# Attention in a macaron layer: the two narrowest diagonal key blocks as one step, the two narrowest maxima blocks in shared banks

## The chip, the cores and the metric

One core of one Trainium2 chip. The metric is the time of one launch on the device in microseconds. Before the change: 1210.66 us, median of 3 runs (1209.63 to 1210.69).

## The reference

Four sequences of 1024 tokens, 512 channels, 16 heads of 32 channels, fp32. A half-weighted feedforward, attention, and the half-weighted feedforward again, each after a layernorm without scale:

```python
x = x + 0.5 * ffn(layernorm(x), weight, bias)
x = x + attn(layernorm(x), Wqkv, bqkv, Wo, bo)
x = x + 0.5 * ffn(layernorm(x), weight, bias)
# ffn: w = clip(round(weight / mean|weight|), -1, 1) * mean|weight|;  x @ w.T + bias
# attn: kqv = x @ Wqkv + bqkv, 16 heads
#   scores = k q^T / sqrt(32); of the 1024 x 1024 the upper triangle is kept,
#   below it -10000; softmax over the axis that is summed against v (causal)
#   out = attn^T v;  out @ Wo + bo
```

## The kernel before

Everything runs in one program in which each engine's order is fixed by tables of rows. A sequence is a batch `b` (4 of them); its heads come in 4 head groups `g` of 4 heads. A head group's attention is done in 2 chunks `c` of 512 queries (`CW`), and a chunk in steps, one for each block of 128 keys up to the diagonal: 4 steps for chunk 0, 8 for chunk 1, `STEPS` = 12. Each step is a slot. 192 slots follow a head of 19 rows, and 10 tail rows follow them.

In a slot TensorE (PE) does, in this order:
- the scores of the step (`scores`, L1137): for each of 4 heads 3 matmuls of split operands (high and low parts), 32 rows of the array per head, so that four heads run side by side, into 4 banks of PSUM; then one matmul per head that adds the row of maxima (L1143);
- the values of the step before (`values`, L1159): 4 matmuls, each head into its own 32 partitions of bank 7;
- a block of maxima (A, L1107): 128 queries against up to 512 keys of the next head group (12 slots hold the 12 blocks of a group), again 3 matmuls for each of 4 heads, into 4 banks;
- then what the row of the table names: P is a piece of K or Q (12 matmuls of 512 columns, L1047), V a tile of values, O an output projection, F1 and F2 the feedforwards (8 matmuls, L1072), T1, T2, T3 transposes (L1064), M and N transposes of maxima and inverses, C the spread of inverses over the heads.

On ScalarE (ACT) a slot has the exponentials of its scores (`exponentials`, L981, one instruction per head, from PSUM to `prob`), high parts of what was multiplied, and the exponentials of the maxima block with their sums (`block_sums`, L953). VectorE (DVE) takes the maxima (`maximum`, L800), low parts (`low`), normalisations, residuals and layernorm statistics. GpSimd (POOL) zeroes the part of `prob` past the diagonal with an affine select (L701), adds biases and computes the inverse roots. SyncE (SP) issues the DMAs: loads and stores of x, weights, and the rows of maxima and inverses (`rows`, `inverse_rows`), which go from 16 partitions to the layout that L1143 and C read.

Seven banks form a ring. Scores take 4, an A block 4, other uses 1. A use waits in `bank_free` until the holder of its bank is done with it: of eight banks for scores and A one is shared in a slot, so that A's fourth bank waits for the first exponential of the slot's own scores, and the next scores' fourth bank for the first maximum of A. `prob` has two buffers, so exponentials of step n wait for the values of step n-2.

Diagonal steps are narrower. In `scores` a block is computed at least 256 queries wide, and an A block at least 256 keys wide:

```python
c, kb = (0, i) if i < QPC else (1, i - QPC)   # step_of
return c, kb, max(0, P * kb - CW * c)
off = min(off, 2 * P)                          # scores
n = CW if kc < c else max(2 * P, P * (r + 1))  # A blocks
```

So the last two steps of a chunk have scores of 256 and 256, exponentials of 256 and 128, values of 256 and 128 columns. The first two diagonal A blocks have matmuls of 256 and maxima of 128 and 256.

Of the kernel before, what the change touches and what calls it, by code (L numbers as in the profile page):

```python
# [30 lines left out]
STEPS = QPC + 2 * QPC  # L31
# [4 lines left out]
VG = GROUPS - 1  # L36


def step_of(i):

    c, kb = (0, i) if i < QPC else (1, i - QPC)
    return c, kb, max(0, P * kb - CW * c)


def diagonal(i):
    c, kb, _ = step_of(i)
    return kb >= QPC * c


def maxima(b, g, c):  # L50

    return [("A", b, g, QPC * c + r, kc) for r in range(QPC) for kc in range(c + 1)]


def pieces(b, g):
    return [("P", b, g, K_, 0), ("P", b, g, Q_, 0), ("P", b, g, K_, 1), ("P", b, g, Q_, 1)]
# [10 lines left out]
    "N P | A",  # L67
    "M P | A | X3.0",
    "P | A | X3.1",
    "C O.0 | A | X3.2",  # L70
    "O.1 | A",
    "N T3.0 O.2 | A | X3.3",
    "M F2.0 | A",
    "T3.1 O.3 | A | X3.4",
    "F2.1 | A",
    "T3.2 O.4 | A",
    "F2.2 | A",
)
GROUP1_ROWS = (
    "C P | A",  # L80
    "N P | A",
    "M P | A | X3.5",
    "P | A",
    "C T3.3 O.5 | A | X3.6",
    "F2.3 | A",
    "N T3.4 O.6 | A | X3.7",
    "M F2.4 | A",
    "T3.5 O.7 | A",
    "T3.6 F2.5 | A | X1.0",
    "T3.7 F2.6 | A | LV",  # L90
    "F2.7 | A",
)
GROUP2_ROWS = (
    "C P | A | X1.1",
    "N T1.0 P | A | X1.2",
    "M F1.0 | A | X1.3",
    "P | A | X1.4",
    "C T2.0 T1.1 P | A | X1.5",
    "T1.2 F1.1 | A | X1.6",
    "N T1.3 F1.2 | A | X1.7",  # L100
    "M T2.1 T1.4 F1.3 | A",
    "T1.5 F1.4 | A",
    "T2.2 T1.6 F1.5 | A",
    "T1.7 F1.6 | A",
    "T2.3 F1.7 | A",
)
GROUP3_ROWS = (
    "C T2.4 P | A",
    "N T2.5 P | A",
    "M T2.6 V.0 | A",  # L110
# [4 lines left out]
    "M V.3 | A",  # L115
    "V.4 | A",
    "V.5 | A",
    "V.6 | A",
    "V.7 | A",
)  # L120
FIRST_ROWS = (
    "P | A",
    "N P | A | | W",
    "M P | A",
    "P | A | | W",
    "C | A",
    "V.4 | A | | W",
    "N V.5 | A",
    "M V.6 | A | | W",
    "V.7 | A",  # L130
    " | A | | W",
    " | A",
    " | A | | W",
# [3 lines left out]
    "N | A",  # L137
    "M | | X3.0",
# [5 lines left out]
    "T3.1 F2.0",  # L144
    "O.3 | | X3.5",
# [33 lines left out]
    "V.3 | A A A",  # L179
# [73 lines left out]
BLOCKS = {u: n for n, u in enumerate([u for u in USES if u[0] == "A"])}  # L253
# [58 lines left out]
def macaron_kernel(nc, x, wqkv, bqkv, wo, bo, wf, bf, out):  # L312
    with ExitStack() as ctx:
# [309 lines left out]
        def _(pool):  # L623
# [65 lines left out]
            for k, s in enumerate(SLOTS):  # L689
# [4 lines left out]
                if s.step is not None:  # L694
                    i = s.step % STEPS
                    if diagonal(i):
                        n = step(s.b, s.step)
                        off = step_of(i)[2]
                        part = prob[:, n % 2, :, off:off + P]
                        pool.wait_ge(s_exp, 4 * n + 4)  # L700
                        nc.gpsimd.affine_select(out=part, in_=part, compare_op=ALU.is_ge, fill=0.0, base=0,  # L701
                                                pattern=[[0, 4], [1, P]], channel_multiplier=-1).then_inc(masked, 1)
# [11 lines left out]
        def _(dve):  # L714
# [75 lines left out]
            def maximum(u):  # L790

                _, b, g, qb, kc = u
                c, r = qb // QPC, qb % QPC
                n, off = (CW, 0) if kc < c else (P * (r + 1), CW - P * r)
                dve.wait_ge(ring_full, full(u))
                for h in range(4):
                    at = 4 * h + r
                    if BLOCKS[u]:
                        dve.wait_ge(a_free, block_at(u, h) - 4)
                    nc.vector.tensor_tensor_reduce(masked_scores[:, h, 0:n], psum(u, h)[:, 0:n], mask[:, off:off + n],  # L800
                                                   -SCALE, BIG, ALU.add, ALU.min, mst[:, c + kc, at:at + 1])\
                        .then_inc(a_max, 1)
# [7 lines left out]

            def inverse(u):

                _, b, g, c = u
                at = group(b, g)
                if c == 0:
                    dve.wait_ge(a_free, block_at(maxima(b, g, 0)[-1]))
                    of = ssum[:, 0, :]
                else:
                    dve.wait_ge(shift_exp, at)
                    nc.vector.tensor_tensor(msh[:, :, :], msh[:, :, :], ssum[:, 1:3, :], ALU.mult).then_inc(inverse_done, 1)  # L820
                    dve.wait_ge(inverse_done, 4 * at - 2)
                    nc.vector.tensor_tensor(msh[:, 0, :], msh[:, 0, :], msh[:, 1, :], ALU.add).then_inc(inverse_done, 1)
                    dve.wait_ge(inverse_done, 4 * at - 1)
                    of = msh[:, 0, :]
                if ended(u):
                    dve.wait_ge(ring_full, full(("N", b, g, c - 1) if c else ("N", *before(b, g), 1)))
                nc.vector.reciprocal(rcol[:, :], of).then_inc(inverse_done, 1)
# [36 lines left out]
            for k, s in enumerate(SLOTS):  # L864
# [27 lines left out]
        def _(act):  # L892
# [38 lines left out]
            def evacuate(u):  # L931
# [9 lines left out]
                act.wait_ge(value_done, step(b, g * STEPS + (STEPS if c else QPC)))  # L941
                nc.scalar.activation(chunk(b, CHUNKS * g + c), accv[:, :], ACT.Identity).then_inc(accv_free, 1)

            def block_sums(u, heads):

                _, b, g, qb, kc = u
                c, r = qb // QPC, qb % QPC
                n = CW if kc < c else P * (r + 1)
                for h in heads:
                    at = 4 * h + r  # L950
                    act.wait_ge(a_max, block_at(u, h))
                    of = masked_scores[:, h, 0:n]
                    nc.scalar.activation(of, of, ACT.Exp, bias=mst[:, c + kc, at:at + 1], scale=-1.0,  # L953
# [246 lines left out]
```

## Time and profile before

| | |
|---|---|
| median of 3 runs | 1210.66 us |
| the profiled execution | 1212.57 us |
| its span, first to last instruction | 1210.8 us |
| mean granted TensorE clock | 0.952 |
| slots (steps) | 192 |

A page of a profile gives the busy time of each engine, as microseconds and share of the span. The table of stretches gives the same for parts of the span, with the granted clock of TensorE as a share of 2.4 GHz. A timeline lists instructions merged by line: where they start, how long until the last of them ends, and in brackets how long the engine had been idle and what ended that. Ends of matmuls overlap the starts of the next, so a stage is measured from start to start.

### The profile page before, as it was taken

The numbers are of one execution on the slowest core, as the hardware profiler recorded it, in microseconds if no ns is written. First come the engines' busy times: TensorE is split into PE (matmuls) and PEld (weight loads), VectorE is DVE, ScalarE is ACT, GpSimd is POOL, SyncE is SP. The second block draws the span as 40 slices with busy tenths as digits, with TensorE's granted clock in tenths as the row PEclk, the third lists the DMA queues.
The fourth block names the chain that finished last, engine by engine and source line by source line (L and its number), as shares of the span: only waits on it lengthen the run. The fifth ranks groups of instructions, "written<-read, shape, count | busy, mean of one in ns | idle before, by whom it ended". The sixth has DMA issues, their size and how long they took to land.

```text
span 1210.8 us, 26364 instructions
## 1 busy us (share of the span) xinstructions
PE 1143.3 (94%) x9466; PEld 718.4 (59%) x9466; DVE 750.1 (62%) x2304; ACT 946.1 (78%) x2699; POOL 347.0 (29%) x503
## 2 busy tenths in 40 slices
PE   4688999899999999999999999999999999998996
PEld 3465556465666666665666666665666666654555
DVE  6865434479844666779745666779744666654344
ACT  1248887888888888888888888888888888888541
POOL 4821120035401232335401232335301332301243
PEclk9898978789999999999999999999999999997599
DMA  7431311011112211231112211330112212100121
GB/s 252 150 102 54 106 44 48 29 54 54 38 45 71 72 38 54 83 122 54 46 38 71 72 37 61 115 104 33 46 37 71 72 37 72 37 3 2 37 68 38
DMA packets 41969, 77.72 MB, mean 64 GB/s; under 512 B 5488, under 2 KB 11632, under 8 KB 41840
## 3 DMA queue, kind: packets, MB, share of 16 engines
q1 hardware_dynamic: 41840, 76.04, 18.8%
q8 instruction: 76, 1.25, 0.4%
q14 instruction: 53, 0.43, 0.1%
HBM read 49.81 MB, written 25.17 MB: 62 GB/s over the span
## 4 chain that ended last, share of the span: by engine, by line
PE 76%; DVE 10%; ACT 8%; issue 2%; POOL 2%; DMA 1%; SPq 0%; DVEq 0%; ACTq 0%; POOLq 0%
PE bank L1047 27%; PE bank L1107 14%; PE bank L1137 11%; PE bank L1159 10%; PE bank L1072 7%; ACT masked_scores L953 5%; DVE masked_scores L800 4%; PE bank L1064 3%; PE bank L1143 3%; DVE st L749 1%; DVE hn L768 1%; ACT prob L981 1%; DVE qT L776 1%; DVE xt L788 1%; ACT qT L904 1%
## 5 line engine op out<-in xcount | busy, mean ns | idle before, releaser
L800 DVE CUSTOM_DVE_ANT_0 masked_scores<-bank,mask 128x512 f32<-128x512 f32 (+3 forms) x768 | 382.1, 554 | 297.9 <-PE bank L1107 263.2
L953 ACT ACTIVATE masked_scores<-masked_scores,mst 128x512 f32<-128x512 f32 (+3 forms) x768 | 463.7, 610 | 48.1 <-DVE mst L800 47.5
L981 ACT ACTIVATE prob<-bank 128x512 f32<-128x512 f32 (+3 forms) x768 | 311.9, 491 | 40.2 <-PE bank L1143 39.2
L1107 PE MATMUL bank<-kT,qT 32*128 32x512 f32 (+2 forms) x2304 | 203.6, 404 | 14.9 <-ACT prob L981 8.4
L701 POOL TENSOR_SCALAR_AFFINE_SELECT prob<-prob 128x512 f32<-128x512 f32 x128 | 81.5, 637 | 448.5 <-ACT prob L981 447.5
L1107 PEld LDWEIGHTS bank<-kT,qT 32*128 32x128 f32 x2304 | 115.1, 191 | 159.3 <-issue 71.9
L1047 PE MATMUL bank<-hT,wqk 128*128 128x512 f32 x768 | 197.4, 407 | 0.0
L1137 PE MATMUL bank<-qT,kT 32*128 32x512 f32 (+2 forms) x2304 | 185.9, 394 | 5.2 <-DVE mst L800 4.5
L1047 PEld LDWEIGHTS bank<-hT,wqk 128*128 128x128 f32 x768 | 143.2, 193 | 37.6 <-ACT prob L981 7.1
L1137 PEld LDWEIGHTS bank<-qT,kT 32*128 32x128 f32 x2304 | 105.8, 192 | 83.5 <-issue 57.2
L1159 PE MATMUL bank<-prob,v 128*32 128x512 f32 (+3 forms) x1344 | 149.4, 518 | 0.0
L953 ACT ACTIVATION_READ_ACCUMULATOR masked_scores<-masked_scores,mst 128x1 f32 x768 | 148.3, 193 | 0.0
L1072 PE MATMUL bank<-wfT,hts 128*128 128x512 f32 x512 | 136.5, 410 | 1.4 <-DVE hts L774 1.4
L1072 PEld LDWEIGHTS bank<-wfT,hts 128*128 128x128 f32 x512 | 93.6, 193 | 23.9 <-DVE hts L774 2.4
L1047 PE MATMUL bank<-wvo,hts 128*128 128x512 f32 x384 | 99.9, 411 | 5.8 <-POOL hts L674 5.8
L667 POOL TENSOR_TENSOR xt<-xt,hb 128x512 f32<-128x512 f32 x64 | 82.1, 1283 | 60.6 <-DVE hn L768 60.6
L1047 PE MATMUL bank<-wvo,hT 128*128 128x512 f32 x384 | 99.2, 408 | 0.0
L1047 PEld LDWEIGHTS bank<-wvo,hts 128*128 128x128 f32 x384 | 72.5, 195 | 26.1 <-ACT prob L981 6.5
L1047 PEld LDWEIGHTS bank<-wvo,hT 128*128 128x128 f32 x384 | 71.8, 194 | 19.8 <-ACT prob L981 4.0
L918 ACT ACTIVATE hts<-bank 128x512 fp32r<-128x512 f32 x64 | 38.6, 603 | 56.9 <-PE bank L1064 36.0
L1064 PE MATMUL bank<-ident,hn 128*128 128x128 f32 x384 | 61.5, 291 | 19.7 <-DVE hn L768 19.3
L1143 PE MATMUL bank<-mneg,onesr 2*128 2x512 f32 (+2 forms) x768 | 77.8, 358 | 0.0
(87 smaller groups left out, 1008.8 us busy)
## 6 DMA issues: line engine op xcount, KB each, us to landing
wqk<-weight_scratch SPq DMA_DIRECT2D x30, 512.0 KB, 3.3
wvo<-weight_scratch SPq DMA_DIRECT2D x20, 512.0 KB, 6.0
xt<-in_L_attn_x_dram SPq DMA_DIRECT2D x32, 256.0 KB, 3.6
residual_scratch<-xt SPq DMA_DIRECT2D x32, 256.0 KB, 2.0
xt<-residual_scratch SPq DMA_DIRECT2D x32, 256.0 KB, 2.8
out_dram<-xt SPq DMA_DIRECT2D x32, 256.0 KB, 2.0
o<-in_L_attn_Wqkv_dram SPq DMA_DIRECT2D x12, 256.0 KB, 4.7
weight_scratch<-o SPq DMA_DIRECT2D x6, 512.0 KB, 2.9
```

Of the source, the lines that this page charges most:

```text
L667: nc.gpsimd.tensor_tensor(to, to, (bo2 if l == 1 else hb)[:, :], ALU.add).then_inc(xb_done[l], 1)
L701: nc.gpsimd.affine_select(out=part, in_=part, compare_op=ALU.is_ge, fill=0.0, base=0, pattern=[[0, 4], [1, P]], channel_multiplier=-1).the ...
L800: nc.vector.tensor_tensor_reduce(masked_scores[:, h, 0:n], psum(u, h)[:, 0:n], mask[:, off:off + n], -SCALE, BIG, ALU.add, ALU.min, mst[:, ...
L953: nc.scalar.activation(of, of, ACT.Exp, bias=mst[:, c + kc, at:at + 1], scale=-1.0, accum_out=ssum[:, c + kc, at:at + 1]).then_inc(a_free, 1)
L981: nc.scalar.activation(prob[:, at % 2, h, off:CW], psum(("S", b, n), h)[:, off:CW], ACT.Exp, scale=SCALE)\
L1047: m = nc.tensor.matmul(psum(u), left(x, k), right(y, k), start=(n == 0), stop=(n == len(terms) - 1))
L1064: m = nc.tensor.transpose(psum(u)[:, P * k:P * k + P], hn[:, TURN[u] % 2, P * k:P * k + P], ident[:, :])
L1072: m = nc.tensor.matmul(psum(u), h[:, part, k, :], wfT[:, k, :], start=(k == 0 and part == HI), stop=(k == KC - 1 and part == LO))
L1107: m = nc.tensor.matmul(psum(u, h)[:, 0:n], query_piece(b, g, c)[row, x, P * r:P * r + P], kT[g % 2][row, y, CW * kc:CW * kc + n], start=(t ...
L1137: nc.tensor.matmul(psum(u, h)[:, off:CW], kT[g % 2][row, x, P * kb:P * kb + P], query_piece(b, g, c)[row, y, off:CW], start=(term == 0), s ...
L1143: m = nc.tensor.matmul(psum(u, h)[:, off:CW], onesr[row, :], mneg[row, c, off:CW], start=False, stop=True)
L1159: m = nc.tensor.matmul(accv[HD * h:HD * h + HD, off:CW], v_of(b, g, kb, h), prob[:, at % 2, h, off:CW], start=(kb == 0), stop=(kb == QPC * ...
```

## The change

The last two key blocks of a chunk, (2, 3) and (6, 7), become one step. The 4 banks of its scores hold the later block's 256 queries in columns 0 to 255 and the earlier block's in 256 to 511; one exponential per head covers columns 128 to 511, one affine select on POOL zeroes both triangles, and the values follow as 4 matmuls of 256 and 4 of 128 columns. The maxima blocks of the first two diagonal query tiles share 4 banks in the same manner, with a maximum and a sum for each tile as before. A head group has 10 slots and 10 A blocks where it had 12, a launch 160 slots. The tables are written anew: uses of the two dropped rows are spread over the others, some rows hold two products, the first piece of the next weights comes in the last row of a group, N and M share a row. On DVE the first half of the inversion (`combine`) moves from N's slot to that of the second C. Number and size of the matmuls stay.

```diff
-STEPS = QPC + 2 * QPC
+KEYS = [[(0,), (1,), (2, 3)], [(0,), (1,), (2,), (3,), (4,), (5,), (6, 7)]]
+QUERIES = [[(0, (0, 1)), (0, (2,)), (0, (3,))],
+           [(0, (0,)), (0, (1,)), (0, (2,)), (0, (3,)), (1, (0, 1)), (1, (2,)), (1, (3,))]]
+STEPS = sum(CHUNK_STEPS)
...
+    return first_query(c, keys[0]) if len(keys) == 1 else P
...
-    return [("P", b, g, K_, 0), ("P", b, g, Q_, 0), ("P", b, g, K_, 1), ("P", b, g, Q_, 1)]
+    second = (Q_, K_) if g == 0 else (K_, Q_)
...
 GROUP2_ROWS = (
-    "C P | A | X1.1",
-    "N T1.0 P | A | X1.2",
...
+    "C T1.0 F2.7 P | A | X1.3",
+    "N M T1.1 F1.0 P | A | X1.4",
...
-                        part = prob[:, n % 2, :, off:off + P]
+                        part = prob[:, n % 2, :, at:at + m * P].rearrange("p h (m q) -> p h m q", m=m)
...
+                    for j, r, at, n, off in block_tiles(u):
+                        nc.vector.tensor_tensor_reduce(masked_scores[:, h, at:at + n], psum(u, h)[:, at:at + n],
...
+                        for j, r, at, keys, _ in block_tiles(u):
+                            n = max(HALF, keys)
+                            for h in range(4):
+                                if term == 0 and j == 0:
+                                    bank_free(u, h)
...
+                parts = [(kb, min(first_query(c, kb), HALF), HALF - HALF * j if len(keys) > 1 else first_query(c, kb))
+                         for j, kb in enumerate(keys)]
                 for term, (x, y) in enumerate(((HI, HI), (LO, HI), (HI, LO))):
+                    for kb, off, at in parts:
+                        for h in range(4):
...
+                for j, kb in enumerate(keys):
+                    off = first_query(c, kb)
+                    of = off - HALF * j
+                    for h in range(4):
+                        m = nc.tensor.matmul(accv[HD * h:HD * h + HD, off:CW], v_of(b, g, kb, h),
```

PE, the end of batch 1's last head group: the last two steps of chunk 1, before. L1137 are scores, L1143 the row of maxima, L1159 values, L1107 an A block, L1047 a product.

```order
L1137 MATMUL bank<-qT,kT 128x256 x12
L1143 MATMUL bank<-mneg,onesr 128x256 x4
L1159 MATMUL bank<-prob,vx 32x384 x4
L1107 MATMUL bank<-kT,qT 128x512 x12
L1047 MATMUL bank<-wvo,hT 128x512 x12
L1137 MATMUL bank<-qT,kT 128x256 x12
L1143 MATMUL bank<-mneg,onesr 128x256 x4
L1159 MATMUL bank<-prob,vx 32x256 x4
L1107 MATMUL bank<-kT,qT 128x384 x12
```

The same place now, as far as the values of the merged step (L1162 scores, L1170 the row of maxima, L1190 values, L1128 an A block, L1066 a product).

```order
L1162 MATMUL bank<-qT,kT 128x256 x24
L1170 MATMUL bank<-mneg,onesr 128x256 x8
L1190 MATMUL bank<-prob,vx 32x384 x4
L1128 MATMUL bank<-kT,qT 128x384 x12
L1066 MATMUL bank<-hT,wqk 128x512 x12
L1162 MATMUL bank<-qT,kT 128x512 x12
L1170 MATMUL bank<-mneg,onesr 128x512 x4
L1190 MATMUL bank<-prob,vx 32x256 x4
L1190 MATMUL bank<-prob,vx 32x128 x4
```

Two stages of 12 and two of 4 became one of 24 and one of 8, and the values of the two key blocks follow each other in the next slot.

DVE, the third head group of batch 1, behind the maxima of one slot (hts and hT are low parts of T1 and T2, hn a normalisation, xt a residual, BN statistics). Before, in the slot with T1.5 and F1.4:

```order
L774 TENSOR_TENSOR hts<-bank,hts 128x512
L768 TENSOR_SCALAR hn<-xt,mv,rstd 128x512 x2
L788 SCALAR_TENSOR_TENSOR xt<-bank,small,xt 128x512
L749 BN_STATS st<-xt 128x6
L751 BN_AGGR mv<-st 128x2
L749 BN_STATS st<-xt 128x6
L751 BN_AGGR mv<-st 128x2
```

Now, in the slot with T2.0, T1.4 and F1.3:

```order
L792 TENSOR_TENSOR hT<-bank,hT 128x4x128
L792 TENSOR_TENSOR hts<-bank,hts 128x512
L786 TENSOR_SCALAR hn<-xt,mv,rstd 128x512 x2
L806 SCALAR_TENSOR_TENSOR xt<-bank,small,xt 128x512
L767 BN_STATS st<-xt 128x6
L769 BN_AGGR mv<-st 128x2
L767 BN_STATS st<-xt 128x6
L769 BN_AGGR mv<-st 128x2
```

The fifth slot of that group now has both low parts beside the two normalisations and both statistics.

## Rows read from the trace of the kernel before

**Rows 1.** The page: busy time of each engine, share of the span, instructions.
```profile
PE 1143.3 (94%) x9466; PEld 718.4 (59%) x9466; DVE 750.1 (62%) x2304; ACT 946.1 (78%) x2699; POOL 347.0 (29%) x503
```
**Rows 2.** Stretches: us, then busy time of PE, weight loads, DVE, ACT, POOL; clock, DMA.
```profile
104.19:241.94 137.75, 128.60 (x1014) 73.16 (x1014) 60.65 (x229) 112.97 (x328) 18.72 (x23) 0.82 0.16 56
241.94:1055.97 814.03, 806.20 (x7085) 509.81 (x7082) 550.38 (x1723) 703.02 (x2017) 242.21 (x353) 0.99 0.18 60
1055.97:1113.10 57.13, 53.60 (x486) 30.53 (x489) 28.98 (x108) 51.20 (x151) 4.72 (x8) 0.92 0.02 7
1113.10:1145.30 32.20, 30.63 (x189) 15.89 (x185) 9.42 (x32) 20.50 (x57) 5.74 (x9) 0.50 0.12 35
516.27:584.73 68.46, 66.44 (x601) 42.03 (x600) 59.93 (x177) 58.91 (x168) 32.02 (x50) 1.00 0.22 76
```
**Rows 3.** Timeline of PE: start us, length us, line, count [idle before <-releaser].
```profile
562.88 0.97 PE L1137 MATMUL bank<-qT,kT 32*128 32x512 f32 x12
563.68 0.41 PE L1143 MATMUL bank<-mneg,onesr 2*128 2x512 f32 x4
564.02 1.06 PE L1159 MATMUL bank<-prob,v 128*32 128x512 f32 x8
565.01 0.97 PE L1107 MATMUL bank<-kT,qT 32*128 32x512 f32 x12
565.91 0.66 PE L1064 MATMUL bank<-ident,hn 128*128 128x128 f32 x4
...
568.35 0.80 PE L1137 MATMUL bank<-qT,kT 32*128 32x384 f32 x12
...
574.92 0.85 PE L1159 MATMUL bank<-prob,v 128*32 128x384 f32 x8
575.70 1.52 PE L1107 MATMUL bank<-kT,qT 32*128 32x512 f32 x12
...
579.58 0.63 PE L1137 MATMUL bank<-qT,kT 32*128 32x256 f32 x12
580.04 0.28 PE L1143 MATMUL bank<-mneg,onesr 2*128 2x256 f32 x4
580.25 0.64 PE L1159 MATMUL bank<-prob,v 128*32 128x256 f32 x8
580.82 0.44 PE L1107 MATMUL bank<-kT,qT 32*128 32x384 f32 x2
...
582.29 0.66 PE L1064 MATMUL bank<-ident,hn 128*128 128x128 f32 x4
...
639.90 0.63 PE L1107 MATMUL bank<-kT,qT 32*128 32x256 f32 x12
640.45 3.01 PE L1047 MATMUL bank<-wvo,hT 128*128 128x512 f32 x12
...
655.18 0.42 PE L1159 MATMUL bank<-prob,vx 128*32 128x128 f32 x8
655.53 1.15 PE L1107 MATMUL bank<-kT,qT 32*128 32x512 f32 x11
```
**Rows 4.** Groups by shape, ACT's exponentials: count | busy us, mean ns | idle before, releaser.
```profile
L981 ACT ACTIVATE prob<-bank 128x384 f32<-128x384 f32 x128 | 51.9, 492 | 1.6 <-PE bank L1143 1.6
L981 ACT ACTIVATE prob<-bank 128x256 f32<-128x256 f32 x128 | 38.3, 384 | 4.3 <-PE bank L1143 4.2
L981 ACT ACTIVATE prob<-bank 128x128 f32<-128x128 f32 x128 | 24.6, 277 | 4.8 <-PE bank L1143 4.7
```
**Rows 5.** The same view, POOL's select.
```profile
L701 POOL TENSOR_SCALAR_AFFINE_SELECT prob<-prob 128x512 f32<-128x512 f32 x128 | 81.5, 637 | 448.5 <-ACT prob L981 447.5
```
**Rows 6.** Timeline of DVE, one slot of the third group of batch 1.
```profile
566.03 0.69 DVE L800 CUSTOM_DVE_ANT_0 masked_scores<-bank,mask 128x512 f32<-128x512 f32 x1 [0.38 <-PE bank L1107]
...
568.48 0.69 DVE L774 TENSOR_TENSOR hts<-bank,hts 128x512 fp32r<-128x512 f32 x1
...
572.42 0.42 DVE L800 CUSTOM_DVE_ANT_0 masked_scores<-bank,mask 128x256 f32<-128x256 f32 x1
```

More of the change, by code:

```diff
@@ L50, in maxima @@
+DIAGONALS = [i for i in range(STEPS) if diagonal(i)]
 def maxima(b, g, c):
-    return [("A", b, g, QPC * c + r, kc) for r in range(QPC) for kc in range(c + 1)]
+    return [("A", b, g, c, kc, tiles) for kc, tiles in QUERIES[c]]
 def pieces(b, g):
-    return [("P", b, g, K_, 0), ("P", b, g, Q_, 0), ("P", b, g, K_, 1), ("P", b, g, Q_, 1)]
+    second = (Q_, K_) if g == 0 else (K_, Q_)
+    return [("P", b, g, K_, 0), ("P", b, g, Q_, 0)] + [("P", b, g, j, 1) for j in second]
 GROUP0_ROWS = (
     "C P | A | LO",
-    "N P | A",
@@ L68 @@
-    "M P | A | X3.0",
+    "N M P | A | X3.0",
     "P | A | X3.1",
     "C O.0 | A | X3.2",
[L71 to L77, printed above, removed]
+    "O.1 | A | X3.3",
+    "N T3.0 O.2 | A",
+    "M F2.0 | A | X3.4",
+    "T3.1 O.3 | A",
+    "T3.2 F2.1 | A | X3.5",
+    "F2.2 P | A",
 )
 GROUP1_ROWS = (
-    "C P | A",
-    "N P | A",
-    "M P | A | X3.5",
+    "C T3.3 P | A | X3.6",
+    "N M F2.3 P | A | X3.7",
@@ L114 @@
     "N V.2 | A",
-    "M V.3 | A",
-    "V.4 | A",
+    "M V.3 V.4 | A",
     "V.5 | A",
-    "V.6 | A",
-    "V.7 | A",
+    "V.6 V.7 | A",
+    "P | A",
 )
 FIRST_ROWS = (
-    "P | A",
[L123 to L133, printed above, removed]
+    "P P | A",
+    "N M P | A | | W",
+    "P | A | | W",
+    "C V.4 | A | | W",
+    "V.5 | A | | W",
+    "N V.6 | A | | W",
+    "M V.7 | A | | W",
+    " | A",
+    " | A",
+    "P | A",
 )
@@ L178 @@
     "M V.2 | A | | W",
[L179 removed]
+    "V.3 | A A",
     " | A A | | W",
@@ L400, in split, with block_at, block_tiles @@
             return SPLIT[u] + 1
-        def block_at(u, h=3):
-            return 4 * BLOCKS[u] + h + 1
+        def block_at(u, h=3, j=None):
+            return COUNTED[u] + h * len(u[5]) + (len(u[5]) if j is None else j + 1)
+        def block_tiles(u):
+            _, b, g, c, kc, tiles = u
+            return [(j, r, HALF * j, CW if kc < c else P * (r + 1), 0 if kc < c else CW - P * r)
+                    for j, r in enumerate(tiles)]
         def tile(b, t):
@@ L871, in _ @@
                         inverse(u)
+                    elif u[0] == "C" and u[3] == 0:
+                        combine(u)
                 if s.step is None:
```

166 lines of the change are left out of this document (80 added, 86 removed).

## The prediction

> **What bounds the kernel now.** Start with the busy times [rows 1]: TensorE (PE) is at work for 94% of the span, ScalarE (ACT) 78%, VectorE (DVE) 62%, GpSimd (POOL) 29%. An average hides stages, so read the table of stretches next [rows 2] and see three kinds of time. From 241.94 to 1055.97 us, twelve head groups in 814.03 us, PE is busy for 806.20: PE sets the pace. From 104.19 to 241.94 (the first two groups, 24 slots, few products in them) the granted clock is 0.82 and ACT is busy for 112.97 of 137.75 us, idle 24.8, about 1.03 us in each slot: here the loop of scores, exponentials and maxima sets the pace, a slot costing ACT's work plus that latency. From 1055.97 to 1113.10 (the last batch's third group, 12 slots) it is the same with 5.9 us idle, 0.49 a slot. The third group of batch 1 (516.27 to 584.73) is special: DVE is busy for 59.93 of 68.46 us, because the residual and its statistics of the next batch's first feedforward lie there.
>
> Then read PE's timeline for what one stage costs, from its start to the start of the next [rows 3]. Scores: 0.80 us at 512 queries (562.88 to 563.68), 0.46 at 256 (579.58 to 580.04). The row of maxima added to them (L1143): 0.34 at 512, 0.21 at 256. Values: 0.57 at 256 (580.25 to 580.82), 0.35 at 128 (655.18 to 655.53), 0.78 at 384 (574.92 to 575.70). Maxima block (A, L1107): 0.90 at 512 (565.01 to 565.91), 0.55 at 256 (639.90 to 640.45). The reader is to see that halving the columns does not halve the stage. Each stage has an entry fee of 0.1 to 0.2 us (scores 0.12, row of maxima 0.08, values 0.13 to 0.14, maxima 0.20) beside its columns. One row is no clean stage: the A block of 384 at 580.82 takes 1.47 us, where the widths beside it would give about 0.73; it waits for a bank and for DVE.
>
> **The change part by part.** Matmuls, their columns, products and transposes stay as many as before. What goes is entries.
>
> *Merged stages, PE-paced time.* I price a merged stage by the row that moves the same columns behind one entry. Scores: 2 x 0.46 become 0.80, saves 0.12. Row of maxima: 2 x 0.21 become 0.34, saves 0.08. Values: 0.57 + 0.35 become 0.78, the 384 row, saves 0.14. Two A blocks of 256 (the diagonal one is issued 256 wide in both versions) become one of 512 columns per head: 2 x 0.55 to 0.90, saves 0.20. Sum 0.54 us, twice in a head group, 1.08; twelve groups: **13.0 us** [rows 3]. Bounds: 0 if a second piece in the same bank pays its own entry; 13.0 is the top. I take the top, since within a stage the rounds already follow each other with no entry, and a second piece is only three more rounds.
> The Trainium skill (TensorE: Matmul & The Clock Gate, section "Back-to-back issue gap") gives a single matmul's spacing as its columns at the clock plus about 2.5 ns. Read as a rule for stages it knows no entry fee: this term would be near 0 instead of 13.0 and the forecast about 1200. The trace disagrees with that reading: by it the 256-wide scores would take half of the 512-wide, and they take 0.46 against 0.80.
>
> *Waits for a bank.* Where a narrow values stage (0.35, 0.57) stands ahead of A, the exponentials that free A's fourth bank are late (the 1.47 row). A merged values stage is longer (0.78) and covers more of them. But the diagonal slots were also those in which ACT had little to do, and two of them are gone, so ACT and DVE have less room to catch up. Bounds per group: +1.0 lost, 1.5 gained (two waits like the 0.74 at 580.82). I take 0.3 in nine groups (the third ones apart): **2.7 us**.
>
> *ACT.* Exponentials of 256 and of 128 columns (38.3 us and 24.6 us for 128 each, 0.299 and 0.192) become one of 384 (51.9 / 128 = 0.405) [rows 4]: 0.086 each, 8 in a group, 0.7 us per group. In PE-paced time this is hidden and worth nothing. The blocks of the maxima keep their instructions on ACT and DVE: 768 each.
>
> *First two groups and the last batch's third.* Here a slot's latency counts. Two slots fewer in each group: 4 x 1.03 = 4.1, and 2 x 0.7 = 1.4: **5.5 us** (bounds 1.4, only ACT's work, to 9). The last batch's third group: 2 x 0.49 + 0.7 = **1.7 us**. Last group (from 1113.10, clock 0.50 at first): no maxima left to merge, two pairs at 0.34, one of them at half clock: **1.0 us**. Head and tail products: same work, 0.
>
> *Mask.* Two selects of 4 x 128 (81.5 us for 128, 0.637 each [rows 5]) become one of twice the elements; bounds 0.64 and 1.3 us, I take 1.3. Values of the pair wait for it in the next slot, but both pair slots of every group up to the last carry a product behind the A block, and the next slot's scores and row of maxima (1.14) come first. Exponentials 1.6 plus mask 1.3 are 2.9 us, against 0.78 + 0.73 + 2 at least + 1.14 = 4.6 of PE work. Nothing is charged. Without that cover it would cost about 0.3 us a pair.
>
> *Combining the sums* moves on DVE from the slot that inverts to the slot of the second C; its exponential was issued three slots before, so no new wait. Row DMAs on SP (maxima, inverses) keep two slots, over 10 us, ahead of their use; the X loads are issued earlier, behind stores that were also issued earlier. Nothing charged; a late X load would show as DVE idle.
>
> *The third group of a batch, three times.* Eight F and eight T1 uses now fall in ten slots, so three neighbours (the fourth to sixth) carry the whole DVE load. The slot that begins on DVE at 566.03 holds that load, four maxima of 512, T low part, two normalisations, F and two statistics, in 6.39 us to 572.42 [rows 6]. The three slots add to it a second low part (0.6 to 0.7) or C's product and the combination (1.0): about 7.4 + 7.0 + 6.9 = 21.3 us. PE needs for them about 5.7 + 5.9 + 6.0 = 17.6 (5.47 for the slot at 562.88 to 568.35, and the added transposes and C at about 0.4). So DVE costs PE 3.7 us there. The same group of before also stalls: the A block at 575.70 runs 1.52 where a clean one shows 0.97, the one at 580.82 takes 1.47 for some 0.73. That is 1.3 us in two of its eight DVE-laden slots; over all eight I estimate 4. Net **0**, bounds 3.7 lost and 3 won per group.
>
> Sum: 13.0 + 2.7 + 5.5 + 1.7 + 1.0 = 23.9. The profiled execution took 1212.57 us (span 1210.8, 1.8 around it), which becomes 1188.7. The median of the runs shown is 1210.66, 1.9 lower; against it the forecast is **1186.7 us**.
>
> **The rivals.**
> *DVE jam.* The third groups lose 3.7 us each and win back nothing of the old stalls; ACT, with the same work in fewer slots, eats the 2.7. For: DVE is 88% busy there already [rows 2]. Against: seven of ten slots stay PE-paced. 1186.7 + 11.1 + 2.7 = about 1200.
> *More than forecast.* Shorter starved stretches also let the clock rise. At 0.82 over 137.75 us, about 50 us were at half speed (1.2 GHz), at 0.92 and 0.50 another 41. If half of them went and half of that were PE-paced, 45 / 2 / 2 = 11 more: about 1175.
> *No change.* The second pieces pay full entries (minus 13.0) and masks and bank waits take about 10 more: 1210.
> *Slower: the clock falls in the third groups.* Place: their fourth to sixth slots, where PE has 17.6 us of work in 21.3. Before, 1.0 was granted there. If the clock drops to 1.2 GHz and stays low through the starved slots, each microsecond at half clock loses half a microsecond of work. The gain of 24 is gone at 48 us of it, 16 per group. With 25 us in each of three groups the price is 37.5: 1224. For: the stretches at 0.82 and 0.50 are the ones where PE waited for ACT. Against: PE kept 1.00 through a group in which DVE was busy 88% [rows 2]. The Trainium skill (same page, "HAM oscillation — how this bites in real kernels") says that pauses between bursts bring the half clock back; no row of the third groups shows it so far.
>
> **How the numbers follow.** Chances: forecast 0.58 (own range 1180 to 1194), DVE jam 0.17, more than forecast 0.10, no change 0.06, slower 0.09. A measurement of this kernel can tell 0.2% (2.4 us) from no change. So faster 0.85, same 0.06, slower 0.09. The range takes in the jam and the larger gain, 1174 to 1203, and leaves out the last two cases and little more.
>
> **What would show it.** PE's timeline should have scores of 24 matmuls at about 0.80, L1170 with 8 at 0.34, the pair's values at 0.78, A blocks of 24 at 0.90. Twelve groups should take about 798 us for 814, the first two about 132 for 137.75, the clock no lower. A pair stage at 0.92 instead of 0.80 refutes the first term. DVE without gaps and PE waiting at A in the third groups is the jam; a granted clock under 1.0 there is the slower case; waits of the values for POOL would refute the free mask.

## The result and the profile after

The changed kernel takes 1166.89 us (median of 4 runs, 1165.19 to 1167.17), the kernel before 1210.68 beside it on the same chip (4 runs, 1209.63 to 1217.03). The ratio is 0.9625, with a 95% interval of 0.9591 to 0.9659: 43.8 us faster. The forecast was 1186.7 us and 24 faster, its range ended at 1174. The sign was right, the size was not, and neither was the range.

First a line of the page of the kernel after: busy times and instructions of each engine.
```profile
PE 1098.4 (94%) x9466; PEld 709.0 (61%) x9466; DVE 739.8 (64%) x2304; ACT 930.6 (80%) x2571; POOL 344.1 (30%) x471
```
PE issues 9466 matmuls, as in [rows 1], and is busy for 44.9 us less. Neither columns nor matmuls went, so what went is time between and inside stages. ACT lost 15.5 us, 11 of them forecast (0.7 in each of 16 groups).

The stretches of the kernel after, with the columns of [rows 2]: the first two groups; three stretches of four groups; the last batch's third group; its last group, in four parts.
```profile
102.33:235.73 133.40, 126.82 (x1021) 74.83 (x1018) 63.43 (x242) 114.44 (x328) 20.87 (x22) 0.83 0.18 61
235.73:495.98 260.25, 257.69 (x2353) 167.59 (x2353) 179.13 (x571) 229.53 (x636) 79.10 (x104) 1.00 0.19 64
495.98:758.06 262.08, 259.53 (x2361) 168.97 (x2361) 179.89 (x572) 229.86 (x636) 80.20 (x112) 1.00 0.20 67
758.06:1021.49 263.43, 260.82 (x2361) 170.17 (x2360) 178.81 (x569) 230.47 (x644) 78.17 (x109) 0.99 0.17 56
1021.49:1075.75 54.26, 49.88 (x484) 28.02 (x483) 28.49 (x106) 49.23 (x140) 3.82 (x5) 0.97 0.04 13
1075.75:1093.44 17.69, 16.60 (x164) 8.99 (x161) 6.50 (x25) 14.07 (x38) 3.56 (x4) 0.71 0.13 46
1093.44:1101.75 8.31, 5.98 (x26) 3.46 (x22) 0.69 (x1) 3.91 (x10) 2.83 (x4) 0.79 0.02 5
1101.75:1128.36 26.61, 26.61 (x214) 17.02 (x213) 12.70 (x24) 13.04 (x29) 13.35 (x19) 1.00 0.12 41
1128.36:1163.40 35.04, 24.23 (x122) 18.23 (x121) 16.36 (x27) 5.77 (x13) 13.83 (x20) 0.99 0.17 61
```
The last group of the kernel before, cut at the same places (the output of its first chunk's sums, the scores behind the first product after it, the end of the last scores' slot):
```profile
1113.14:1136.21 23.07, 22.16 (x164) 11.29 (x164) 8.73 (x31) 16.60 (x49) 2.87 (x5) 0.50 0.16 48
1136.21:1145.32 9.11, 8.45 (x33) 4.56 (x25) 0.69 (x1) 3.90 (x10) 2.83 (x4) 0.51 0.01 2
1145.32:1174.57 29.25, 27.75 (x223) 17.21 (x222) 13.20 (x26) 13.34 (x33) 13.56 (x20) 1.00 0.11 37
1174.57:1210.80 36.23, 25.46 (x114) 19.21 (x113) 16.35 (x27) 5.77 (x13) 13.79 (x20) 0.94 0.18 59
```
From this the ledger of the span (1210.8 to 1163.4) is made, each difference beside its term of the forecast:

| stretch | before, us | after, us | difference | forecast |
|---|---|---|---|---|
| ahead of the first group | 104.19 | 102.33 | -1.9 | 0 |
| first two groups | 137.75 | 133.40 | -4.4 | -5.5 |
| next four groups | 274.33 | 260.25 | -14.1 | -5.2 |
| next four | 269.73 | 262.08 | -7.7 | -5.2 |
| next four | 269.97 | 263.43 | -6.5 | -5.2 |
| last batch's third group | 57.17 | 54.26 | -2.9 | -1.7 |
| last group and tail | 97.66 | 87.65 | -10.0 | -1.0 |

The two profiled executions are 47.4 us apart and the medians 43.8, so 3.6 us of this table belong to these two executions and not to the change.

The new tables also moved work across the borders of the stretches, and the rows have to be compared like for like. One product of 12 matmuls went from the last batch's third group (48 such matmuls before, 36 after) into the first two groups (144 and 156). One feedforward piece of 8 matmuls, 2.0 us, went from the first stretch of four groups (128 and 120) into the last batch's third group (0 and 8).

- *First two groups:* they gained 4.4 with a product more, which takes 4.38 us there, most of it at 1.2 GHz; so 8.7 like for like, or 7.3 with a product at its 2.94 of full clock.
```profile
231.35 4.45 PE L1066 MATMUL bank<-hT,wqk 128*128 128x512 f32 x12
```
- *Next four groups:* 14.1 less 2.0 is 12.1. They began, before, with a slot of 10.17 us at a granted clock of 0.56 (241.94 to 252.11); the same slot after takes 6.40 (235.73 to 242.13), with 0.41 of transposes that the other had not. That is 4.2 us; 7.9 remain, beside 7.7 in the next four.
- *The 6.5 of the last four* hold a loss of 1.6 in one slot at half clock (shown below), so 8.1 without it.
- *Last batch's third group:* a piece more and a product less are 1.0 us less work, so its 2.9 are 1.9.

Now PE's timeline of three slots of the kernel after, to be read from start to start as [rows 3].
```profile
572.33 0.80 PE L1162 MATMUL bank<-qT,kT 32*128 32x384 f32 x12
...
574.30 1.05 PE L1128 MATMUL bank<-kT,qT 32*128 32x256 f32 x24
575.28 0.28 PE L1143 MATMUL bank<-ident,rcol 128*16 128x128 f32 x1
...
579.03 0.39 PE L1162 MATMUL bank<-qT,kT 32*128 32x256 f32 x4
...
585.29 0.97 PE L1162 MATMUL bank<-qT,kT 32*128 32x512 f32 x12
...
586.43 0.86 PE L1190 MATMUL bank<-prob,vx 128*32 128x256 f32 x16
587.21 0.97 PE L1128 MATMUL bank<-kT,qT 32*128 32x512 f32 x12
588.03 0.38 PE L1147 MATMUL bank<-rall,pick 8*128 8x512 f32 x1
588.34 3.01 PE L1066 MATMUL bank<-hT,wqk 128*128 128x512 f32 x12
...
1124.00 0.98 PE L1162 MATMUL bank<-qT,kT 32*128 32x256 f32 x24
1124.81 0.40 PE L1170 MATMUL bank<-mneg,onesr 2*128 2x256 f32 x8
1125.15 0.85 PE L1190 MATMUL bank<-prob,vx 128*32 128x384 f32 x8
```
The merged stages are where the forecast put them: scores of 24 in 0.81 (1124.00 to 1124.81; forecast 0.80), the row of maxima of 8 in 0.34, the pair's values of 16 in 0.78 (586.43 to 587.21), the maxima block of 24 in 0.98 here and 0.92 at its shortest (forecast 0.90). One row is new: the 512-wide block behind the pair's values takes 0.82 (587.21 to 588.03), where it took 0.99 in the middle of such slots before, and the C behind it 0.31 for 0.45.

Adding all stages of the second stretch of four groups by kind, from start to start, tells what a batch gained: maxima blocks 43.8 to 41.4, products 126.6 to 124.7, values 38.4 to 36.5, C, M and N 5.5 to 4.1, scores and row of maxima 45.5 to 45.3, transposes 10.0 to 10.2; together -7.65. Scores and row of maxima saved 0.2 in each of eight pairs, and gave most of it back in the third group, where PE now waits for DVE:
```profile
526.19 1.24 PE L1162 MATMUL bank<-qT,kT 32*128 32x512 f32 x11
...
533.23 1.19 PE L1162 MATMUL bank<-qT,kT 32*128 32x512 f32 x11
```
From the start of the scores to that of the values, three slots there (526.19, 533.23 and 547.15) take 1.63, 1.58 and 1.44 us for 1.14: 1.2 us in all. DVE's own timeline shows the cause, a slot with nothing idle in it, from its first maximum to the start of the next slot:
```profile
531.09 0.69 DVE L817 CUSTOM_DVE_ANT_0 masked_scores<-bank,mask 128x512 f32<-128x512 f32 x1
...
538.05 0.23 DVE L845 RECIPROCAL rcol<-msh 128x16 f32<-128x16 f32 x1
```
The three jammed slots took DVE 6.98, 6.96 and 6.83 us (524.11 to 544.88); 7.4, 7.0 and 6.9 were forecast.

In the third group of batch 2 (758.06 to 829.26) the same jam met the clock. Behind a wait of 1.01 us for DVE at 800.50 the granted clock of the 6 us from 800 is 0.72, which is 3.4 us at 1.2 GHz, and eight matmuls that take 2.03 elsewhere take 3.23:
```profile
801.83 3.31 PE L1091 MATMUL bank<-wfT,hts 128*128 128x512 f32 x8
```
That slot takes 9.77 us, and 8.17 in the same group of batch 1, where the clock stayed at 1.00.

### The profile page after: what moved, and what is told of

The parts are those of the page before. It is cut to its first block, busy times and chain, and to the rows that moved or that the text cites. A ratio compares the mean times of both kernels' runs of the same rounds, so it can differ in the third digit from the quotient of the medians.

```text
span 1163.4 us, 26100 instructions
## 1 busy us (share of the span) xinstructions
PE 1098.4 (94%) x9466; PEld 709.0 (61%) x9466; DVE 739.8 (64%) x2304; ACT 930.6 (80%) x2571; POOL 344.1 (30%) x471
## 4 chain that ended last, share of the span: by engine, by line
PE 78%; ACT 10%; DVE 7%; issue 2%; POOL 2%; DMA 1%; SPq 0%; DVEq 0%; ACTq 0%; POOLq 0%
PE bank L1066 30%; PE bank L1128 12%; PE bank L1190 11%; PE bank L1162 10%; PE bank L1091 7%; ACT masked_scores L972 6%; PE bank L1083 3%; PE bank L1170 3%; DVE masked_scores L817 2%; ACT prob L1000 2%; DVE st L767 1%; DVE hn L786 1%; POOL xt L685 1%; POOL rstd L675 1%; PE bank L1143 1%
## 5 line engine op out<-in xcount | busy, mean ns | idle before, releaser
L1000 ACT ACTIVATE prob<-bank 128x512 f32<-128x512 f32 (+1 forms) x640 | 300.1, 553 | 23.9 <-PE bank L1170 23.4
L719 POOL TENSOR_SCALAR_AFFINE_SELECT prob<-prob 128x512 f32<-128x512 f32 (+1 forms) x96 | 78.8, 821 | 414.9 <-ACT prob L1000 414.6
L1066 PE MATMUL bank<-hT,wqk 128*128 128x512 f32 x768 | 194.4, 403 | 0.0
L1128 PE MATMUL bank<-kT,qT 32*128 32x512 f32 (+2 forms) x2304 | 179.9, 387 | 15.1 <-ACT prob L1000 11.7
L1128 PEld LDWEIGHTS bank<-kT,qT 32*128 32x128 f32 x2304 | 104.7, 189 | 138.1 <-issue 66.7
L1162 PE MATMUL bank<-qT,kT 32*128 32x512 f32 (+2 forms) x2304 | 176.6, 382 | 3.1 <-DVE mst L817 2.4
L1066 PEld LDWEIGHTS bank<-hT,wqk 128*128 128x128 f32 x768 | 144.0, 192 | 38.9 <-ACT prob L1000 8.1
L1162 PEld LDWEIGHTS bank<-qT,kT 32*128 32x128 f32 x2304 | 102.2, 188 | 71.0 <-issue 45.9
L1190 PE MATMUL bank<-prob,v 128*32 128x512 f32 (+3 forms) x1344 | 142.8, 513 | 0.0
L1066 PE MATMUL bank<-wvo,hts 128*128 128x512 f32 x384 | 97.3, 403 | 6.0 <-POOL hts L692 6.0
L1066 PE MATMUL bank<-wvo,hT 128*128 128x512 f32 x384 | 95.8, 401 | 0.0
L1066 PEld LDWEIGHTS bank<-wvo,hts 128*128 128x128 f32 x384 | 70.9, 191 | 25.8 <-ACT prob L1000 7.3
L1066 PEld LDWEIGHTS bank<-wvo,hT 128*128 128x128 f32 x384 | 71.2, 191 | 17.4 <-ACT prob L1000 1.4
L1170 PE MATMUL bank<-mneg,onesr 2*128 2x512 f32 (+2 forms) x768 | 72.3, 354 | 0.8 <-DMA mneg<-mrow 0.8
```

Of the source, the lines that this page charges most:

```text
L1000: nc.scalar.activation(prob[:, at % 2, h, off:CW], psum(("S", b, n), h)[:, off:CW], ACT.Exp, scale=SCALE)\
L1066: m = nc.tensor.matmul(psum(u), left(x, k), right(y, k), start=(n == 0), stop=(n == len(terms) - 1))
L1128: m = nc.tensor.matmul(psum(u, h)[:, at:at + n], query_piece(b, g, c)[row, x, P * r:P * r + P], kT[g % 2][row, y, CW * kc:CW * kc + n], st ...
L1162: nc.tensor.matmul(psum(u, h)[:, at:at + CW - off], kT[g % 2][row, x, P * kb:P * kb + P], query_piece(b, g, c)[row, y, off:CW], start=(ter ...
L1170: m = nc.tensor.matmul(psum(u, h)[:, at:at + CW - off], onesr[row, :], mneg[row, c, off:CW], start=False, stop=(kb == keys[-1]))
L1190: m = nc.tensor.matmul(accv[HD * h:HD * h + HD, off:CW], v_of(b, g, kb, h), prob[:, at % 2, h, of:of + CW - off], start=(kb == 0), stop=(k ...
```

## The experiments

The theory after the result had three parts. (a) The change works through two things at once: fewer slots, and fewer takings of the seven banks by maxima blocks. (b) A stage's fee is not paid by a stage as such, but for something at its border. (c) What the starved stretches gained beyond their slots is the clock. The rival of (a) is that the parts add up, each worth its share; that of (c), that latency alone did it.

### One half of the change: ten slots, maxima not shared

The tables of the change, but blocks of maxima one per query tile again; two of them stand in rows 2 and 9 of each group.
```diff
-           [(0, (0,)), (0, (1,)), (0, (2,)), (0, (3,)), (1, (0, 1)), (1, (2,)), (1, (3,))]]
+           [(0, (0,)), (0, (1,)), (0, (2,)), (0, (3,)), (1, (0,)), (1, (1,)), (1, (2,)), (1, (3,))]]
...
-    "N M P | A | X3.0",
+    "N M P | A A | X3.0",
```


> Ten slots in a head group as in the change, but the two narrowest maxima blocks in banks of their own again: 12 A blocks, two in each of two slots of a group. Theory (a stage's entry is what merging saves): A blocks of 256 cost 0.55 each for a merged 0.92, so 32 x 0.19 = 6 us, 1173. Second theory (banks count too): the second block's fourth bank waits for VectorE's first maximum of the first, some 0.3 to 0.5 us each time, 10 to 16 us more, about 1183. If A's sharing were worth nothing: 1167.

Measured: 1201.05 us (1195.86 to 1205.40), ratio 0.9928 [0.9902, 0.9954]. Of 43.8 us only 9 are left, less than any of the three expectations allowed. PE's timeline of the slot with two blocks, to be set beside the one at 572.33 above:
```profile
582.58 0.80 PE L1162 MATMUL bank<-qT,kT 32*128 32x384 f32 x12
...
584.55 1.84 PE L1128 MATMUL bank<-kT,qT 32*128 32x256 f32 x24
586.32 0.28 PE L1143 MATMUL bank<-ident,rcol 128*16 128x128 f32 x1
...
588.79 3.04 PE L1066 MATMUL bank<-wvo,hT 128*128 128x512 f32 x12 [1.64 <-DVE mst L817]
```
The same 24 matmuls of 256 take 1.77 us instead of 0.98, and the product behind them waits 1.64 for a bank that the second block holds until DVE has read it. The slot takes 9.18 us, to the next scores at 591.76, for 6.70. The larger part of the second block's price is not at the block but at the next taker of a bank.

### The other half: shared maxima in twelve slots

The tables of the kernel before with the shared blocks (ten in a group; rows 2 and 4 have none); every key block is its own step.
```diff
+KEYS = [[(k,) for k in range(QPC)], [(k,) for k in range(2 * QPC)]]
...
+QUERIES = [[(0, (0, 1)), (0, (2,)), (0, (3,))],
+           [(0, (0,)), (0, (1,)), (0, (2,)), (0, (3,)), (1, (0, 1)), (1, (2,)), (1, (3,))]]
```


> Twelve slots as before, tables as before, but the A blocks shared: 10 A blocks, two slots of a group without one. Theory (most of the gain comes from merged steps and fewer slots): A's sharing alone gives 3 to 6 us on before, 1205 to 1208. Rival (A's banks are what holds PE, fewer bank takes give most): 1180 or less.

Measured: 1223.17 us (1221.06 to 1224.07), ratio 1.0108 [1.0084, 1.0132]: slower than before, and neither expectation had that. The slots without a block shrink (4.20 us for 5.14), but the last three of a group grow (5.24, 5.34 and 5.33 for 4.90, 4.80 and 4.65). Its waits:
```profile
PE bank L1140 <- ACT prob L1012: 13.7, 20, 2.0
PE bank L1174 <- DVE mst L829: 7.2, 14, 0.7
```
In the kernel before the two are 8.4 and 4.5 us, in the kernel after 11.7 and 2.4. So -9 for fewer slots alone, +13 for sharing alone, and -44 together: with these tables the parts do not add. In ten slots, twelve blocks leave two slots with two. In twelve slots, ten blocks leave two slots with none, and no slot of a group has two. The kernel before had one block in each slot, like the kernel after, so evenness alone is not the gain: it is what the gain of ten slots needs.

Where the sharing lost, the stretches tell. The nine PE-paced groups, the third ones left out, took 0.5 us more in all; the third groups of the first three batches 4.8 more, the first two groups 3.2, the last batch's third group 4.1 (57.17 to 61.29), and what is ahead of the first group 1.5, while the last group won 3.4. The loss is thus where ACT or DVE is short of time; that it comes from the lumps of work of a shared block is my reading and not shown. Each half was run with one table alone. Whether other places for the empty or the double slots would have made the halves better was not tried.

This run says more about the last group, which I had priced at 1.0 us. Between the two outputs of sums there (`o<-bank` on ACT: the previous group's last chunk, this group's first) lie 17.60 us in the kernel before, 13.60 here, and 12.41 after:
```profile
1132.68 0.60 ACT L974 ACTIVATE o<-bank 128x512 f32<-128x512 f32 x1
...
1146.28 0.63 ACT L974 ACTIVATE o<-bank 128x512 f32<-128x512 f32 x1
```
Same twelve slots, 4.0 us less than before: one block of maxima remains there and not two. Up to 1.0 of the 4.0 may be the clock, which was 0.72 here and 0.50 before; with filler matmuls and a clock of 0.76 the kernel before took 16.61 (below). The slot fewer makes another 1.2; the run with ten slots and blocks unshared, which also has one block there, took 12.85. Why a block matters so much is on DVE's timeline of the kernel before: the second block's last maximum is read at 1127.36, the column of maxima follows it, then the row goes through PE, ACT and a DMA to the scores of the next chunk.
```profile
1125.52 0.69 DVE L800 CUSTOM_DVE_ANT_0 masked_scores<-bank,mask 128x512 f32<-128x512 f32 x1 [3.22 <-PE bank L1107]
...
1127.36 0.69 DVE L800 CUSTOM_DVE_ANT_0 masked_scores<-bank,mask 128x512 f32<-128x512 f32 x1
...
1128.09 0.17 DVE L805 TENSOR_TENSOR mcol<-mst 128x16 f32<-128x16 f32 x1
```

### Does a second piece pay an entry?

The kernel after with the merged step's stages issued one key block after the other: scores 256, row 256, scores 256, row 256.
```diff
-                for term, (x, y) in enumerate(((HI, HI), (LO, HI), (HI, LO))):
-                    for kb, off, at in parts:
+                for kb, off, at in parts:
+                    for term, (x, y) in enumerate(((HI, HI), (LO, HI), (HI, LO))):
```


> The changed kernel, with the scores and the row of maxima of a merged step issued key block by key block: 12 matmuls of 256, 4 of the row, 12, 4, in place of 24 and 8. Same work, same exponentials, same slots. Theory (entry fees): each merged step pays 0.12 + 0.08 us again, 32 times, 6.4 us where PE sets the pace in 27 or so of them: 1172 to 1173.5. Rival (entries are free, slots count): 1167.

Measured: 1165.62 us (1162.04 to 1167.11), ratio 0.9609 [0.9582, 0.9635]; the kernel after has 0.9625 [0.9591, 0.9659]. Nothing lost. The rows:
```profile
579.10 0.63 PE L1162 MATMUL bank<-qT,kT 32*128 32x256 f32 x12
579.56 0.29 PE L1169 MATMUL bank<-mneg,onesr 2*128 2x256 f32 x4
579.67 0.53 PE L1162 MATMUL bank<-qT,kT 32*128 32x256 f32 x12
580.03 0.29 PE L1169 MATMUL bank<-mneg,onesr 2*128 2x256 f32 x4
580.25 0.85 PE L1189 MATMUL bank<-prob,vx 128*32 128x384 f32 x8
```
From start to start 0.46, 0.11, 0.36 and 0.22: 1.15 us, as much as 0.81 + 0.34 merged. The 256-wide scores cost 0.46 behind a product and 0.36 behind a row of maxima. The row costs 0.22 ahead of values and 0.11 ahead of scores. So no stage pays a fee for being a stage: about 0.1 us falls where a stage of another form of operands begins (product to scores, row to values, values to maxima), and none between scores and row, which both use the array in four parts of few rows. The amounts of the forecast hold; their reason was wrong. What saves is not the merged instruction run but that two slots' changes of form become one.

### Values split around the block

The kernel after, but the pair's second key block comes behind the maxima block.
```diff
+                    if len(step_of(done[1] % STEPS)[1]) == 2 and s.blocks:
+                        values(*done, 0)
+                        for u in s.blocks:
+                            use(u)
+                        values(*done, 1)
```


> The changed kernel, with the values of a merged step's second key block issued behind the A block: one more change between array layouts (32-row tiles to 32-column tiles) in 32 slots, same matmuls. Theory (the fee is paid where the layout changes, not for each line or stage): 0.13 us x 32 = 4 us slower, 1169 to 1172, and the two pieces take 0.57 and 0.35 again. Rival (no such fee): 1165 to 1167.

Measured: 1179.35 us (1178.88 to 1180.82), ratio 0.9744 [0.9722, 0.9765]. It costs 12.5 us, three times what I expected. The slot is the one at 585.29 above:
```profile
590.16 0.97 PE L1162 MATMUL bank<-qT,kT 32*128 32x512 f32 x12
...
591.30 0.64 PE L1194 MATMUL bank<-prob,vx 128*32 128x256 f32 x8
591.87 1.16 PE L1128 MATMUL bank<-kT,qT 32*128 32x512 f32 x12
592.96 0.43 PE L1194 MATMUL bank<-prob,vx 128*32 128x128 f32 x8
593.32 0.50 PE L1147 MATMUL bank<-rall,pick 8*128 8x512 f32 x1
593.74 3.02 PE L1066 MATMUL bank<-hT,wqk 128*128 128x512 f32 x12
```
The two values cost 0.57 + 0.36 for 0.78, as the forecast's 0.14. But the block now takes 1.09 for 0.82, and C 0.42 for 0.31. The wide values do a second job: they cover the time until ACT has freed the block's bank. ACT's first exponential of the slot begins at 591.43 and takes 0.52. The block's first three matmuls start at 591.87, its fourth at 592.08; in the kernel after all four start at 587.21. In this slot that is 0.27 + 0.11 us beside the 0.15 of the change of form: of the saving, under a third had been in the first term of my sum.

### Is the rest the clock? Filler matmuls

Four kernels repeat nine score matmuls at the start of a step (their results are overwritten by the true ones), in the slots where PE waits for ACT. All have the same edit, with another condition.
```diff
+                            if h == 0 and STARVED(b, n):
+                                for f in range(3):
+                                    bank_free(u, f)
+                                for again in range(3):
+                                    for f in range(3):
...
+                                        nc.tensor.matmul(psum(u, f)[:, off:CW], kT[g % 2][rf, x, P * kb:P * kb + P],
```
On the kernel before, last batch's third group only:

> The kernel before, with repeated first-term score matmuls (9 per slot, overwritten by the real ones) in the starved slots of the last batch's third head group, ahead of the fourth head's bank wait. Theory (the clock fell to 1.2 GHz from 1104.2 to 1145.2 us because PE was starved, and PE-paced slots behind it then ran at half speed, which is some 8 us of the change's gain at the end): the low stretch shrinks, time 1202 to 1206. Rival (the low clock cost nothing, ScalarE set the pace): 1210 to 1214, even where the clock rises.

Measured: 1213.87 us (1211.28 to 1215.68), ratio 1.0027 [1.0012, 1.0043], as the rival had it. The long stretch at 1.2 GHz stayed: it began at 1104.9 and took 41.0 us, as before. On the kernel after, at both ends:

> The changed kernel, with the same filler in its starved slots: the first two head groups' and the last batch's third. Theory (clock): half-clock time there falls from 44 and 17 us, 3 to 6 us faster, 1161 to 1164. Rival: the filler delays scores as much as the clock gives back, 1166 to 1170.

Measured: 1162.13 us (1161.65 to 1165.74), ratio 0.9616 [0.9586, 0.9645]; the mean granted clock of the profiled execution is 0.981 for 0.967. On the kernel before, at both ends and into the last group:

> The kernel before, with the filler matmuls in the starved slots of the first two head groups and of the last batch's third and fourth. Theory (part of what the change gained beyond the forecast is the clock): half-clock time falls from 119 to under 90 us and the first two groups with the slot behind them (which took 10.17 us where its like take 5.83) lose 5 to 8 us: 1202 to 1206. Rival (the clock is worth nothing here, the filler costs as in the earlier run): 1210 to 1215.

Measured: 1212.91 us (1210.63 to 1214.06, 12 runs), ratio 1.0017 [1.0006, 1.0028], with a clock of 0.970 for 0.952. The stretches of this kernel, from the slot behind the first two groups on; then the last batch's third group, and the last group in the parts used above:
```profile
239.11:248.70 9.59, 9.12 (x54) 5.64 (x50) 6.38 (x20) 7.15 (x19) 2.24 (x5) 0.64 0.00 0
...
1052.39:1113.56 61.17, 56.78 (x588) 34.81 (x588) 28.91 (x108) 51.80 (x151) 4.75 (x8) 0.89 0.02 7
1113.56:1135.64 22.08, 19.15 (x213) 11.45 (x209) 8.73 (x31) 16.59 (x48) 2.87 (x5) 0.76 0.14 47
1135.64:1142.38 6.74, 4.40 (x26) 2.33 (x22) 0.69 (x1) 3.91 (x10) 2.84 (x4) 1.00 0.04 12
...
1171.60:1209.40 37.80, 26.97 (x114) 20.37 (x113) 16.45 (x27) 5.77 (x13) 13.78 (x20) 0.91 0.16 56
```
This table settles most of it. The first part of the last group has a clock of 0.76 for 0.50, and takes 22.08 us for 23.07: it is not PE that paces it. The kernel after takes 17.69 at 0.71. So about 1.0 of the 5.4 us won there may be the clock. The second part holds a product that PE does pace: 6.74 us at 1.00, 9.11 at 0.51, and 8.31 at 0.79 after. The product itself takes 2.93, 5.30 and 4.51, so 0.8 of the change's gain is the clock's. The filler wins 2.8 us in the first groups, 0.6 in the slot behind them and 3.4 in the last group, and costs 4.0 in the third group and 1.6 behind: 1.4 of the span is left, and the median, taken over more runs, shows no gain, as the rival had it.

The last one keeps the filler of the kernel after where it won, the first two groups:

> The changed kernel, with the filler in the starved slots of the first two head groups alone (in the earlier run those groups gained 4.3 us and the last batch's third lost 2). Theory: 1160 to 1162. Rival (the gain came from the other end): 1165 to 1167.

Measured: 1162.86 us (1161.91 to 1164.56), ratio 0.9605 [0.9583, 0.9627], which is 4 us under the kernel after, and the simpler of the two that beat it. The third group starts at 232.06 instead of 235.73, so 3.7 us are seen where they were expected. In the times the gain is likely and not shown. None of its four runs (up to 1164.56) reaches the lowest of the kernel after (1165.19), but the intervals overlap, and the run with the stages in another order, no slower by design or by result, had one execution of 1162.04.

## Why the prediction was wrong in size

**Merged stages, 13.0 us: right in size.** Forecast 0.12, 0.08, 0.14 and 0.20; the medians over the twelve groups give 0.10, 0.10, 0.14 and about 0.2: 4.3 us in four groups, for 4.32 forecast. The top of the bounds was the right end. The reading of the Trainium skill (TensorE: Matmul & The Clock Gate, section "Back-to-back issue gap") by which this term was near 0 is refuted for stages that follow another form of operands. It stands inside a form: behind a row of maxima the 256-wide scores take 0.36, a little under half of the 512-wide stage's 0.80. The reason that I gave for the top of the bounds, no second entry within a stage, also fails: the run that issued the two key blocks as stages of their own lost nothing.

**Waits for a bank, 2.7 us: too small, the step that failed in the middle.** I took 0.3 a group between a loss of 1.0 and a gain of 1.5. Four groups gained 7.9, 7.65 and, without the slot at half clock, 8.1 us. Less the 4.3 of the merged stages that is 3.3 to 3.8, or 0.8 to 0.95 a group, after the 1.2 us that the third group gave back at its scores and row of maxima. Three things make it, and I had seen the first only: the cover of the block's bank wait by wide values, and C's cheaper entry behind it (0.17 + 0.14 in a slot; the split values lost 0.38 by the same two). Values of 384 waited for mask and exponentials before, in most slots (0.87 at the median for the 0.78 of [rows 3]) and do not after: 0.7 in four groups. And with ten slots for the same products two of them stand side by side. That is no wait for a bank but a term that the forecast put at nothing ("products and transposes stay as many as before"). Twice in four groups 24 matmuls take 5.65 us, and two apart 2 x 2.94; six times a feedforward piece and a product take 1.93 + 2.81 for 2.02 + 2.94. Eight pairs at 0.22 or so are 1.8 of the 1.9 us by which products fell in four groups.

**First two groups, 5.5 us: too small, within the bounds.** Measured 7.3 to 8.7 like for like, the bounds were 1.4 and 9.

**The clock, 0 in the forecast, 11 in a rival with a chance of 0.10.** The time at 1.2 GHz fell from 118.9 to 77.7 us. Rows show 4.2 us of gain in the slot at 241.94, 0.8 in the first product of the last group, 1.6 in a product of the tail and 1.6 in one ahead of the first group. They also show losses: the product at 231.35 costs 4.38 for 2.94, since the half clock now lies ahead of the third group and not in its first slot (1.4), and the slot at 795.29 costs 1.6. That leaves 5.2, and up to 1.0 in the first part of the last group. Where such stretches fall differs between executions, so this is the account of these two. The rival had the mechanism, and about twice the price, because most of the half-clock time lies where ACT sets the pace: the filler brought back 45 us of full clock in the kernel before and no time.

**Last group, 1.0 us: the step that failed worst.** It gained 10.0. I wrote that it had "no maxima left to merge". It had two blocks (rows 1 and 2 of its table), and has one. I counted PE's stage costs in a stretch where a chain sets the pace: maxima, column, row, DMA, scores, exponentials, sum, output. That chain is shorter by the second block (4.0 with up to 1.0 of clock in it, by the run with twelve slots and shared maxima), by one slot of the first chunk (1.2), and by 0.2 ahead of it: 5.4. The first product has 0.8. The middle part has six slots for seven (29.25 to 26.61, 2.6): a product there waited 1.22 for GpSimd and does not any more, and one pair is merged. What follows the last scores has 1.2. There a product took 4.42 us at 1192.22 before, at half clock, and 2.82 at 1146.41 after, which is 1.6; the first values, now a pair, take 0.4 more. It is no gain of the change: the run with the stages in another order, with the same tail, had 4.41 for that product.

**Ahead of the first group, 0 in the forecast: 1.9.** The last two slots there held five blocks of maxima and hold four; they took 10.8 us (93.38 to 104.19) and take 8.2 (94.13 to 102.33). Of these 2.6, 1.6 are a product at 97.29 that met half the clock in this execution (4.51 us for 2.95), and 1.0 is left for the block fewer. In the other two runs that changed the blocks the same two slots take 8.0 with four blocks (97.75 to 105.70, twelve slots in a group) and 9.9 with five (96.17 to 106.03, ten slots). Up to those slots the kernel after is 0.7 later, so 1.9 remain.

**Last batch's third group, 1.7 us: right.** Measured 2.9, and 1.9 like for like.

**Mask, nothing charged: right.** The select over the pair takes 1.10 us, where I took 1.3, and the weight loads of the values waited 1.2 us in all for the select, where they waited 1.0 before.

**Third groups, net 0: roughly right.** The jam came as priced, 20.8 us of DVE for 21.3. At scores and row of maxima it cost PE 1.2. PE idles there for 1.7 us (68.19 busy of 69.92 us, 495.98 to 565.90), before it was 2.0 [rows 2]. The stall that went and the one that came cancel, as guessed. The group takes 1.5 us more than before and holds a feedforward piece and a transpose more, 2.4 us. The slower case was not empty either: the granted clock stayed at 1.00 in the third group of batch 1, but fell once in that of batch 2, behind a wait for DVE. Its price was 1.6 us in one slot, where the rival had 12.5 in each of three groups.

What could have been known: that a group now has ten blocks in ten slots stood in the change. I priced the halves one by one, and the two experiments with one half each show +13 and -9, where the whole has -44. A sum of parts priced apart did not give that.

## What to carry to other kernels

Where a ring of buffers (here seven banks) is shared by several kinds of work, the number of takings per slot can matter more than the work in them. Keep it even when the number of slots changes: here either change alone gave little or lost. In a stretch that a chain paces, price the chain's links and ask of each which work stands ahead of it; stage costs of the busy engine say nothing there. And a stage that looks too long may be what hides the wait of the next.

## What the runs showed of the hardware

The cost of a border between matmul stages depends on the form of operands on its two sides: 0.10 to 0.15 us between four-part scores (32 rows by 128 columns), column-part values (128 by 32) and full products, by the rows of this case, and none between scores and row of maxima, nor between the scores of two key blocks, as 0.46 beside 0.36 shows. Two products side by side save 0.23 us (5.65 for 2 x 2.94).

One select over 128 x 1024 elements took 1.10 us, and two of 128 x 512 take 1.27 [rows 5]. The group of the kernel after, by shape:
```profile
L719 POOL TENSOR_SCALAR_AFFINE_SELECT prob<-prob 128x1024 f32<-128x1024 f32 x32 | 35.3, 1102 | 115.3 <-ACT prob L1000 115.3
```
Nine added matmuls in each of eight slots raised the mean granted clock of the changed kernel from 0.967 to 0.973, and its third group began 3.7 us earlier. The same trick over a longer stretch of the kernel before bought more full clock and no time. What stays open is why its filler in the third group alone left the 41 us at 1.2 GHz as they were.
